# A conditioned transformer block on Trainium2: x also laid out with features as rows

## What is computed

```python
tp = (silu(cond) @ Wt + bt)[:, None, :]
shift_msa, scale_msa, gate_msa, shift_mlp, scale_mlp, gate_mlp = split(tp, 6)
h = layernorm(x, g1, be1) * (1.0 + scale_msa) + shift_msa
h = attention(h, Wqkv, bqkv, Wproj, bproj)              # 16 heads of 32
x = x + gate_msa * h
h = layernorm(x, g2, be2) * (1.0 + scale_mlp) + shift_mlp
x = x + gate_mlp * (gelu(h @ W1 + b1) @ W2 + b2)
# then: cq = quantised cond; wq = w_proj rounded to -1, 0, 1 times mean |w_proj|
scale, shift = split(cq @ wq.T + b_proj, 2)
out = rmsnorm(x, rms_weight) * (1.0 + scale) + shift
```

## Time and profile before

| | before |
|---|---|
| median of 3 runs | 3829.83 us (3828.05 to 3830.34) |
| profiled execution | 3829.9 us |
| its span, first to last instruction | 3828.1 us |
| PE busy | 3797.0 us, 99% |
| DVE busy | 2412.6 us, 63% |
| ACT busy | 1806.7 us, 47% |
| POOL busy | 2012.4 us, 53% |
| stage 1 ends at about | 615 us |

### The profile page before, as it was taken

How to read it: one execution, slowest core, us unless ns; L and a number is a source line. 1 busy time by engine, 2 the same in 40 slices (tenths; PEclk the granted TensorE clock), 3 DMA queues, 4 the chain that set the end, 5 groups by cost and what they waited for, 6 DMA issues and landing times.

```text
span 3828.1 us, 50208 instructions
## 1 busy us (share of the span) xinstructions
PE 3797.0 (99%) x18707; PEld 2638.1 (69%) x18707; DVE 2412.6 (63%) x4029; ACT 1806.7 (47%) x3229; POOL 2012.4 (53%) x683
## 2 busy tenths in 40 slices
...
GB/s 235 200 178 164 178 222 143 150 152 156 141 162 161 157 144 159 164 157 145 158 165 157 142 162 136 84 36 45 39 50 41 67 45 36 45 36 45 36 45 23
DMA packets 203711, 455.75 MB, mean 119 GB/s; under 512 B 16532, under 2 KB 55508, under 8 KB 187340
## 3 DMA queue, kind: packets, MB, share of 16 engines
...
## 4 chain that ended last, share of the span: by engine, by line
PE 96%; DVE 2%; issue 0%; DMA 0%; ACT 0%; POOL 0%; SPq 0%; POOLq 0%; DVEq 0%; ACTq 0%
PE psum L1159 13%; PE psum L634 13%; PE psum L1173 12%; PE psum L513 10%; PE psum L515 10%; PE psum L514 10%; PE psum L1814 6%; PE psum L1810 6%; PE psum L1812 6%; PE psum L1200 4%; PE psum L1186 1%; DVE max_part L979 1%; PE psum L1763 1%; PE psum L567 1%; PE psum L642 0%
## 5 line engine op out<-in xcount | busy, mean ns | idle before, releaser
L979 DVE TENSOR_REDUCE max_part<-psum 128x1 f32<-128x512 f32 x2048 | 1262.7, 683 | 125.2 <-PE psum L634 113.8
L1415 POOL TENSOR_TENSOR probs_round<-probs_round,probs_round 128x2048 f32<-128x2048 f32 x189 | 888.4, 4701 | 29.3 <-PE psum L1173 24.3
L634 PE MATMUL psum<-k_stack,q_stack 96*128 96x512 f32 x2048 | 775.2, 407 | 6.0 <-DVE max_part L979 2.3
L1159 PE MATMUL psum<-q_stack,k_stack 98*128 98x512 f32 x2048 | 771.9, 412 | 1.9 <-ACT probs L1293 1.1
L1979 DVE TENSOR_TENSOR g_parts<-g_full,g_parts 128x512 fp32r<-128x512 f32 x256 | 259.9, 1015 | 805.0 <-ACT g_parts L1868 805.0
L1293 ACT ACTIVATE probs_round<-psum 128x512 f32<-128x512 f32 x1024 | 543.1, 612 | 385.7 <-PE psum L1159 385.6
L1293 ACT ACTIVATE probs<-psum 128x512 f32<-128x512 f32 x1024 | 551.2, 598 | 140.1 <-PE psum L1159 88.2
L1415 POOL TENSOR_TENSOR probs_round<-probs_round,probs 128x2048 f32<-128x2048 f32 x124 | 568.7, 4586 | 9.7
L1864 ACT ACTIVATE g_full<-psum,cols 128x512 f32<-128x512 f32 x256 | 176.6, 690 | 802.5 <-PE psum L515 802.1
L1159 PEld LDWEIGHTS psum<-q_stack,k_stack 98*128 98x128 f32 x2048 | 377.5, 189 | 241.9 <-ACT probs_round L1293 67.3
L634 PEld LDWEIGHTS psum<-k_stack,q_stack 96*128 96x128 f32 x2048 | 382.3, 189 | 212.2 <-DVE max_part L979 148.0
...
## 6 DMA issues: line engine op xcount, KB each, us to landing
probs<-probs POOLq DMA_DIRECT2D x126, 1024.0 KB, 8.3
qk_parts<-qk_out SPq DMA_DIRECT2D x128, 512.0 KB, 3.3
k_stack<-qk_parts SPq DMA_DIRECT2D x96, 512.0 KB, 6.8
q_stack<-qk_parts SPq DMA_DIRECT2D x192, 256.0 KB, 7.2
x_in<-in_x SPq DMA_DIRECT2D x16, 1024.0 KB, 5.4
v_rows<-v_out SPq DMA_DIRECT2D x64, 256.0 KB, 2.0
v_group<-v_rows SPq DMA_DIRECT2D x32, 512.0 KB, 10.4
gated_attention<-gated SPq DMA_DIRECT2D x64, 256.0 KB, 2.9
```

Source lines behind the costliest of these rows:

```text
L634: pe.matmul(psum[:, SMAX[at.turn % 3], :], q_stack[u % 3][0:PARTS, h, i * P:(i + 1) * P], k_stack[G % 2][0:PARTS, h, kh * CH:(kh + 1) * CH ...
L979: dve.reduce_max(max_part[:, n:n + 1], psum[:, SMAX[at.turn % 3], :], AX.X).then_inc(dve_smax, 1)
L1159: pe.matmul(psum[:, ST[n % 3], :], k_stack[G % 2][0:ROWS, h, kt * P:(kt + 1) * P], q_stack[u % 3][0:ROWS, h, :], start=True, stop=True).th ...
L1415: pool.tensor_tensor(total[:, :, :], total[:, :, :], probs(u, kt)[:, :, :], ALU.add).then_inc(pool_sum, 1)
```

## The change

The caller lays some inputs out anew: xT (x with features as rows), w_projT, condT, and all small vectors as columns. Only chunk 0 is still turned by PE (into the buffer of xT's first copy). For the others SP loads x (one buffer, four neighbouring tokens to a partition) and xT (two buffers), both for chunk c + 2 at the start of chunk c. The statistics of chunk c + 2 are made by DVE between the v evictions of steps 8 and 9 of chunk c; mean and root go as 128 x 2 x 4 numbers to DRAM (`store_stats`, behind the store of step 9's v) and come back spread over all 128 partitions (`load_stats`, 0.5 MB, behind step 11's). DVE then subtracts and multiplies on xT directly, two operations for h_full; the shift is added by ACT (as its bias) and in the lo operation. The rows of L582 and L610 use column tiles, so four partial rows have to be added by DVE (`dve_fold_rows`). w_proj is no longer turned, and neither are cond and the small vectors at the start.

The diff, cut to what bears on the time:

```diff
@@ sp_stage1 @@
-            sp.dma_start(cond[:, :], t["cond"]).then_inc(a_cond, 16)
-            sp.dma_start(x_bufs[0][:, :, :], x_chunk(0)).then_inc(a_x[0], 16)
-            for name, at, n in (("bt", 0, 24), ("g1", 24, 4), ("be1", 28, 4), ("g2", 32, 4),
-                                ("be2", 36, 4), ("bqkv", 40, 8), ("b1", 48, KM)):
-                sp.dma_start(vec_rows[at:at + n, :],
...
+            sp.dma_start(condT[:, :, :], t["condT"]).then_inc(a_cond, 16)
+            sp.dma_start(x_in[:, :, :], x_chunk(0)).then_inc(a_x, 16)
+            sp.dma_start(cols[:, :], t["vectors"]).then_inc(a_vec, 16)
...
-            sp.dma_start(x_bufs[1][:, :, :], x_chunk(1)).then_inc(a_x[1], 16)
+            sp.wait_ge(dve_xn, 1)
+            sp.dma_start(x_in[:, :, :], x_rows(1)).then_inc(a_x, 16)
+            load_xT(sp, 1)
...
+            store_stats(sp, 1)
+            load_stats(sp, 1)
             for c in range(NC):
                 b, half = divmod(c, NCH)
-                if 0 < c < NC - 1:
-                    sp.wait_ge(dve_xn, c)
-                    sp.dma_start(x_bufs[(c + 1) % 2][:, :, :],
-                                 x_chunk(c + 1)).then_inc(a_x[(c + 1) % 2], 16)
+                if c + 2 < NC:
+                    sp.wait_ge(dve_norm1, 4 * c + 5)
+                    sp.dma_start(x_in[:, :, :], x_rows(c + 2)).then_inc(a_x, 16)
+                    if c:
+                        sp.wait_ge(dve_centred, c * KD)
+                    else:
+                        sp.wait_ge(pe_feat, KD)
+                    load_xT(sp, c + 2)
...
+                    if c + 2 < NC and i == 1:
+                        store_stats(sp, c + 2)
+                    elif c + 2 < NC and i == 3:
+                        load_stats(sp, c + 2)
...
+        def store_stats(sp, c):
+            sp.wait_ge(dve_mean, c)
+            sp.wait_ge(act_sqrt1, c + 1)
+            sp.dma_start(stat_dram[c].rearrange("(v p t) -> p v t", v=2, t=TT),
+                         packed[:, :, :]).then_inc(a_stat, 16)
+
+        def load_stats(sp, c):
+            sp.wait_ge(a_stat, 16 * c)
+            if c >= 2:
+                sp.wait_ge(dve_full, c * KD)
+            sp.dma_start(spread[:, :], stat_dram[c].partition_broadcast(P)).then_inc(a_spread, 16)
@@ pe_side_work @@
-                    i = pe.matmul(psum[0:B, SIDE, :], siluT[:, kk, 0:B],
-                                  wt[half][:, kk, 2 * D:3 * D], start=kk == 0, stop=kk == KD - 1)
+                    i = pe.matmul(psum[kk * HD:(kk + 1) * HD, SIDE, :], siluT[:, kk, :],
+                                  wt[half][:, kk, 2 * D:3 * D], start=True, stop=True)
@@ pe_stage1 @@
-                    if KD <= j < 2 * KD and not last:
-                        pe_features(pe, c + 1, j - KD)
@@ act_feature @@
-            act.activation(hT[c % 2][0][:, f, :], h_full[n % 2][:, :],
-                           ACT.Copy).then_inc(act_feat, 1)
+            act.activation(hT[c % 2][0][:, f, :], h_full[n % 2][:, :], ACT.Identity,
+                           bias=ln_shift[:, 0, f, c // NCH:c // NCH + 1]).then_inc(act_feat, 1)
@@ dve_feature @@
+            if c:
+                dve.tensor_tensor(h_full[n % 2][:, :], xT_bufs[c % 2][:, f, :], spread[:, 0:CH],
+                                  ALU.subtract).then_inc(dve_centred, 1)
+                dve.wait_ge(dve_centred, n - KD + 1)
+                dve.scalar_tensor_tensor(h_full[n % 2][:, :], h_full[n % 2][:, :],
+                                         ln_scale[:, 0, f, b:b + 1], spread[:, CH:2 * CH],
+                                         ALU.mult, ALU.mult).then_inc(dve_full, 1)
@@ dve_feature_lo @@
-            dve.tensor_tensor(hT[c % 2][1][:, f, :], h_full[n % 2][:, :],
...
+            dve.scalar_tensor_tensor(hT[c % 2][1][:, f, :], h_full[n % 2][:, :],
+                                     ln_shift[:, 0, f, b:b + 1],
+                                     hT[c % 2][0][:, f, :].bitcast(fp32), ALU.add,
+                                     ALU.subtract).then_inc(dve_lo, 1)
...
+        def dve_fold_rows(dve, out, bias, n):
+
+            for k in range(KD):
+                if k:
+                    dve.wait_ge(dve_part, n * (KD - 1) + k)
+                i = dve.tensor_tensor(out, psum[k * HD:k * HD + B, SIDE, :], out if k else bias,
+                                      ALU.add)
+                i.then_inc(dve_part if k < KD - 1 else side_free, 1)
@@ dve_stage1 @@
-                    if j == 1 and 0 < c < NC - 1:
-                        dve_normalise(dve, c + 1)
...
+                    if i == 0 and c + 2 < NC:
+                        dve_statistics(dve, c + 2)
```

More of the change, by code:

```diff
@@ L31, in build_block @@
     RAW = 3 * D // 2
-    WR = t["w_proj"].shape[0] // P
+    WR = t["w_projT"].shape[1] // P
     BT, GAMMA, BETA, BQK, B1 = 0, (24, 32), (28, 36), 40, 48
@@ L130, in build_block @@
         s1 = Region()
-        x_bufs = [s1(f"x_in{i}", [P, TT, D]) for i in range(2)]
-        xn = s1("xn", [P, TT, D], coarse=True)
+        x_in = s1("x_in", [P, TT, D])
+        xT_bufs = [s1(f"xT_in{i}", [P, KD, CH], coarse=True) for i in range(2)]
+        xn = xT_bufs[0]
         wqkv_hi = s1("wqkv_hi", [P, KD, 3 * D], fp32r)
@@ L135, in build_block @@
         h_full = [s1(f"h_full{i}", [P, CH]) for i in range(2)]
+        spread = s1("spread", [P, 2 * CH])
+        packed = s1("packed", [P, 2, TT])
         hT = [(s1(f"hT_hi{i}", [P, KD, CH], fp32r), s1(f"hT_lo{i}", [P, KD, CH], fp32r))
@@ L325, in piece_of, with wp_piece @@
             return (n + 1) * P > RAW
+        def wp_piece(r):
+            k, part = divmod(r, WR // KD)
+            return wp[:, k, part * D:(part + 1) * D]
         def probs(u, kt):
@@ L590, in pe_side_work @@
                           stop=True).then_inc(pe_side, 1)
-            elif k is not None and k >= 15 and k <= 36 and k % 3 == 0:
-                r = k // 3 - 5
-                pe.wait_ge(side_free, 5 + r)
-                pe.wait_ge(dve_side, 12 + 5 * (r + 1))
-                for kk in range(KD):
-                    i = pe.transpose(psum[:, SIDE, kk * P:(kk + 1) * P],
-                                     wp[:, r, kk * P:(kk + 1) * P], ident[:, :])
-                i.then_inc(pe_side, 1)
             elif k == 39:
-                pe.wait_ge(side_free, 13)
+                pe.wait_ge(side_free, 5)
                 pe.wait_ge(dve_side, 62)
@@ L854, in dve_feature @@
             b = c // NCH
-            dve.wait_ge(pe_feat, n + 1)
-            if n == 0:
-                dve.wait_ge(side_free, 1)
+            if c:
+                if f == 0:
+                    dve.wait_ge(a_xT[c % 2], 16 * ((c + 1) // 2))
+                    dve.wait_ge(a_spread, 16 * c)
+            else:
+                dve.wait_ge(pe_feat, n + 1)
+                if n == 0:
+                    dve.wait_ge(side_free, 1)
             if n >= 2:
@@ L860, in dve_feature @@
                 dve.wait_ge(act_feat, n - 1)
-            dve.tensor_scalar(h_full[n % 2][:, :], psum[:, TR[n % 2], :],
-                              ln_scale[:, 0, f, b:b + 1], ln_shift[:, 0, f, b:b + 1], ALU.mult,
-                              ALU.add).then_inc(dve_full, 1)
+            if c:
+                dve.tensor_tensor(h_full[n % 2][:, :], xT_bufs[c % 2][:, f, :], spread[:, 0:CH],
[4 more added lines that the diff above has]
+                                         ALU.mult, ALU.mult).then_inc(dve_full, 1)
+            else:
+                dve.tensor_scalar(h_full[n % 2][:, :], psum[:, TR[n % 2], :],
+                                  ln_scale[:, 0, f, b:b + 1], None, ALU.mult).then_inc(dve_full, 1)
         def dve_feature_lo(dve, c, f):
@@ L883, in dve_side_work @@
                     dve.wait_ge(a_rows, 16)
-                dve.tensor_tensor(rows[:, 0, :], psum[0:B, SIDE, :], row_bias[:, 0, :],
-                                  ALU.add).then_inc(side_free, 1)
+                dve_fold_rows(dve, rows[:, 0, :], row_bias[:, 0, :], half)
                 dve.wait_ge(side_free, k + 1)
@@ L895, in dve_side_work @@
                 for r in (2 * (k - 5), 2 * (k - 5) + 1):
-                    dve.tensor_reduce(small[:, 8 + r:9 + r], wp[:, r, :], axis=AX.X, op=ALU.add,
+                    dve.tensor_reduce(small[:, 8 + r:9 + r], wp_piece(r), axis=AX.X, op=ALU.add,
                                       apply_absolute_value=True).then_inc(dve_side, 1)
```

168 lines of the change are left out of this document (84 added, 84 removed).

## The result

| | before | after |
|---|---|---|
| median | 3828.94 us (3825.25 to 3831.74, 6 runs) | 3887.06 us (3886.18 to 3890.57, 6 runs) |
| ratio to before | | 1.0154, 95% interval 1.0141 to 1.0167 |
| profiled execution, its span | 3829.9, 3828.1 us | 3888.3, 3886.5 us |
| stage 1 ends (first score product of attention) | 615.23 us | 673.77 us |
| PE busy | 3797.0 us, 99% | 3782.0 us, 97% |

The changed kernel is 58 us slower. The forecast was 3855.9 (3808 to 3873): the sign was right, the size half of what came, and the time lies outside the range. All of it arises in stage 1: attention begins 58.5 us later, and behind that nothing changed.

The account below looks back on a forecast made before the run. TensorE, 99% busy, was taken to bound the kernel; the gross 43 us saved would vanish in waits the change opens. Chunk by chunk the changes summed to +26.0 on 3829.9, giving 3855.9 us, range 3808 to 3873.

Parts of the forecast that it names:

- gross gain: TensorE, stage 1: transposes 29.1 us, w_proj groups 3.3, row products 10.2 and some setup removed; 43 us in all.
- the loop: SP's queue: statistics' round trip and loads delay q/k stores, hence step 4's eviction, features and next v1; +26.0 us with other costs.
- r: Time from a chunk's first product to v1's eviction, where the loop's turn starts: 4.8 us, 7.6 with w_proj pieces.
- a feature step: VectorE's work per feature step, longer because h_full becomes two operations: from 2.8 to 3.57 us.
- from v1's eviction to step 4's: Loop term: statistics' store, then spread, x, xT and two q/k stores, before VectorE evicts step 4; 15.3 us, bounds 13.9 and 17.
- Chunk 1: The second L582 waits for VectorE's chain of additions until 35.5 us, then four v steps: 47.3 us against 46.4.
- Chunk 8: Late v1 eviction, 7.6 us, and 4.3 us of quantising cond on VectorE: 41.5 us against 35.5, +6.0.
- The clock: Rival, 12%: TensorE falls to half clock after new waits in chunks 1 and 9, 2 us each; 3860 us.
- Stores not held: Rival, 22%: step 1's store lands before 13.6 us into the chunk, so only small costs stay; 3805 us.
- half of it: Rival, 14%: quicker loads and a short statistics' store make the loop 2 to 3 us less; no change, 3830 us.
- The round trip is slow: Rival, 8%: statistics' store 3.8 us and broadcast read below 400 GB/s, 17 us for 15.3; 3873 us.
- Column tiles: Rows of L582 and L610: 10.2 us saved on TensorE, little left after VectorE's chain of four additions, 2.9 us.

Follow-up runs that it names:

- e1: The changed kernel with the loads of x and xT moved behind the store of step 4; 3826.06 us, ratio 0.9989 to before.
- e5: e1 with w_proj sums and pieces behind steps 0 and 3, side products later, separate banks for second products; 3800.14 us, ratio 0.9917 to before.
- e11: e5 with norm rows' copies first, gate rows in chunk 2 and bias rows loaded early; 3793.34 us, ratio 0.9906 to before.
- e9: The changed kernel with ScalarE copying chunk 1's norm rows ahead of its eviction of steps 3 and 4; 3886.84 us.
- e3: The changed kernel with extra TensorE products in waits to keep the clock up; 3881.75 us.
- e6: The changed kernel with the four row products summed in PSUM as before, one addition instead of four; 3890.91 us.

## Why the mechanism was right and the size wrong

**What bounds the kernel, and the gross gain.** Right. Where nobody holds TensorE, a chunk is 32.6 us, in e1, e5 and e11. Of the gross gain of 43 us, an estimate, e11 shows 35.

**The mechanism.** Right: the loop closed, with its turns read as forecast: r 7.2 for 7.6 with a piece and 4.4 for 4.8 without, a feature step 3.59 us for 3.57 (48.02 to 51.61 in chunk 0), four steps and a piece 17.3 us for 17.1 (298.15 to 315.41). e1 opened it by moving two loads and nothing else.

**The step that failed is one term of the sum: from v1's eviction to step 4's, 15.3 us.** It measured 16.8 to 18.4, 17.6 in the mean of ten chunks. Of the 2.3 us, the statistics' store has 0.8 (2.9 for 2.1) and the way from spread's issue to the landing of step 1's store 1.3 (13.4 for 12.1). I had added 2.9 us and 3.7 MB at 400 GB/s there. In chunk 6 the DMA moved 152, 156, 111, 258 and 287 GB/s in the windows from 284 to 289 and only then 400. Part of that were the stores of steps 10 and 11, 0.5 MB that I had left out; they were issued ahead of spread and landed at 285.81 and 286.60. How the 1.3 us divide between the slow start and these bytes no run shows. The upper bound, 17, lay nearer, but most turns are above it too.

A loop multiplies its term: chunks 3 to 7 are 9.8 us above the forecast and chunks 10 to 13 9.5, since 4.4 + 17.6 + 14.6 = 36.6 is above both 32.6 and the old 34.6. I had these last four down as a gain of 4.7: with 15.3 the loop lets go behind chunk 9 for two chunks and comes back at 34.0 and 34.4. Measured, it comes back at once (33.4, then 37.4, 36.5, 35.8). One sum of the prediction is off as well: by its own terms chunk 3 is 4.8 + 15.3 + 14.3 + 3.75 = 38.2, not 38.8.

**Chunk 0** ended 3.1 us later than forecast (62.6 for 59.5): its first round trip ended at 34.25, not 32.4, and step 1's store landed 13.0 us after that for 12.1.

**Chunk 1 missed a path:** 56.1 for 47.3. I followed the loop on VectorE and forgot what else stands in ScalarE's queue behind an eviction that waits. ScalarE and TensorE in chunk 1 of the changed kernel:

```profile
84.86 0.69 ACT L764 ACTIVATE qk_out<-psum,cols 128x512 fp32r<-128x512 f32 x1 [13.12 <-DMA qk_parts<-qk_out]
85.44 0.59 ACT L786 ACTIVATE ln_rows<-psum 128x512 f32<-128x512 f32 x1
...
86.17 1.94 PE L575 MATMUL psum<-wt,siluT 128*32 128x512 f32 x8 [7.72 <-ACT ln_rows L786]
```

The copy of the norm rows stood behind the eviction of step 3, and TensorE waited 7.7 us for it and then ran at the low clock. e9 shows that this is not worth its length (5.3 us in the chunk, 1 us of the total). Chunk 2 took 32.6 for 35.0, so the two together are 6.5 us above the forecast.

**Chunk 8** took 47.0 for 41.5. I had added cond's quantisation to VectorE's row, but TensorE's transposes of it (L626) stand ahead of the v steps. They waited 8.94 us, until 32.8 us into the chunk:

```profile
390.27 0.57 PE L626 MATMUL psum<-ident,cq 8*128 8x8 f32 x4 [8.94 <-DVE cq L1003]
```

Behind them come four v steps, 10.9 us, and 2.7 us of slow clock: 47. Chunk 9 gave 2.6 of it back.

**The clock**, a rival with 12% and 3860: the mechanism is real and far more frequent than I thought (I priced it at chunks 1 and 9), but e3 gives it 6 us. Its price depends on who holds the chunk: 0.3 us in chunk 7, inside the loop, 2.3 in chunk 8, where TensorE has work of its own, of which chunk 9 took 1.4 back.

**The other rivals.** "Stores not held" (3805) and "half of it" (3830) are out; e1 and e5 are what the first would look like. "The round trip is slow" (8%, 3873) was the closest, and short by 14 us. Its two causes are there, each in part: the statistics' store took 2.9 us, not 3.8, and the DMA was below 400 GB/s behind the broadcast read. Chunk 0 and the loop's chunks 3 to 7 and 10 to 13 are some 22 us above my forecast, chunks 1 and 2 6.5, chunks 8 and 9 3. I had said that a microsecond moves the sum by some 10, which gives 23 for the 2.3 us of the term; that the two figures are so close is in part luck, since r came out 0.4 us shorter a turn and chunks 10 to 13 joined the loop in full.

**Column tiles and the last chunks** went as forecast: no net gain from the tiles (e6), and 5.2 us lost in chunks 14 and 15 for 4.6. Right too is that the start of wproj_lo is what counts: it comes 37.6 us behind the start of chunk 14 before, 42.8 after and 40.5 in e11, and from it to the first score product it is 45.2 to 45.3 us in all three. Why it is still 2.9 us late in e11 is open.
